# Maxima of an attention kernel: a chunk later in the projections, four steps of lead in place of six, and weight scales in three pieces

## What is computed

```python
def _tlin(x, w, s, b):
    return jnp.einsum('bsh,oh->bso', x, w) * s + b
q = split_heads(_tlin(x, w_q, s_q, b_q))      # k and v alike
scores = jnp.einsum('bhqd,bhkd->bhqk', q, k) / jnp.sqrt(jnp.float32(HEAD))
attn = jax.nn.softmax(scores, axis=-1)
ctx = jnp.einsum('bhqk,bhkd->bhqd', attn, v)
...
def fp4_quant_dequant(x):
    xb = x.reshape(shape[:-1] + (shape[-1] // BLOCK, BLOCK))
    scale = jnp.max(jnp.abs(xb), axis=-1, keepdims=True) / 6.0
    scale = jnp.maximum(scale, jnp.float32(1e-12))
    idx = jnp.searchsorted(_MID, jnp.abs(xb / scale))
    return (_GRID[idx] * jnp.sign(xb / scale) * scale).reshape(shape)
...
h = jax.nn.silu(fp4_linear(x, w_gate)) * fp4_linear(x, w_up)
x = _layernorm(x + fp4_linear(h, w_down), axis=-1)
```

## Time and profile before

| | us |
|---|---|
| median of 3 runs | 1972.64 |
| lowest, highest | 1971.41, 1978.06 |
| the profiled execution | 1978.5 |
| its span | 1976.7 |
| projections, up to the first attention maximum | 200.8 |
| attention steps with maxima (490) | 1179.0 |
| attention steps without maxima (22) | 52.5 |
| feed, up to the end | 544.4 |

### The profile page before, as it was taken

One profiled execution on the slowest core, in us unless ns is written; L12 is line 12 of the kernel. 1 busy time (PEld: TensorE's weight loads), 2 busy tenths in 40 slices (PEclk: granted clock), 3 DMA queues, 4 the chain that ended last, 5 costly groups with the idle time before them and its releaser, 6 DMA issues.

```text
span 1976.7 us, 43274 instructions
## 1 busy us (share of the span) xinstructions
PE 1921.4 (97%) x15934; PEld 1130.0 (57%) x15934; DVE 1846.1 (93%) x3237; ACT 1639.0 (83%) x3225; POOL 749.1 (38%) x747
## 2 busy tenths in 40 slices
PE   8999999999999999999999999999999999999998
PEld 7767444444444444444444444444478888888876
DVE  4798999999999999999999999999289999999997
ACT  5555889889898998989899898988967777777776
POOL 3000455666674362010001001000046666666785
PEclk9999999999999999999999999999999999999999
DMA  7985643354445435444543544452011111111210
GB/s 219 287 241 218 124 63 52 62 106 93 86 90 102 94 72 108 91 87 89 104 94 72 103 95 88 88 104 93 24 49 49 49 49 49 50 50 55 62 33 28
DMA packets 127200, 181.48 MB, mean 92 GB/s; under 512 B 37836, under 2 KB 82636, under 8 KB 126988
## 3 DMA queue, kind: packets, MB, share of 16 engines
q1 hardware_dynamic: 119308, 171.10, 37.3%
q10 hardware_dynamic: 7392, 7.34, 1.2%
q0 software_dynamic: 288, 0.27, 0.1%
HBM read 103.68 MB, written 73.40 MB: 90 GB/s over the span
## 4 chain that ended last, share of the span: by engine, by line
DVE 64%; PE 31%; issue 3%; DMA 1%; ACT 1%; SPq 0%; DVEq 0%; POOLq 0%; POOL 0%; ACTq 0%
DVE halfmax L1135 50%; PE ps L1401 11%; DVE halfmax L1130 7%; PE ps L1440 6%; PE ps L493 4%; PE ps L1389 2%; PE ps L505 2%; PE ps L1412 2%; PE ps L1045 1%; PE ps L1011 1%; PE ps L1448 1%; PE ps L480 1%; DVE room L1591 1%; PE ps L1457 1%; DVE room L1678 1%
## 5 line engine op out<-in xcount | busy, mean ns | idle before, releaser
L1096 ACT ACTIVATE room<-ps 128x512 f32<-128x512 f32 x2048 | 1085.0, 601 | 123.3 <-PE ps L1011 101.5
L1135 DVE TENSOR_REDUCE halfmax<-ps 128x1 f32<-128x512 f32 x1714 | 1040.3, 680 | 0.1
L1011 PE MATMUL ps<-qs,ks 50*128 50x512 f32 x2048 | 715.9, 448 | 2.4 <-DVE halfmax L1135 1.3
L986 PE MATMUL ps<-ks,qs 48*128 48x512 f32 x1960 | 667.0, 436 | 23.8 <-DVE halfmax L1130 22.4
L1045 PE MATMUL ps<-room,vals 128*17 128x256 f32 (+2 forms) x8192 | 578.2, 384 | 0.3 <-ACT craw L1104 0.3
L986 PEld LDWEIGHTS ps<-ks,qs 48*128 48x128 f32 x1960 | 314.2, 184 | 423.4 <-DVE halfmax L1135 308.1
L164 POOL CAST mrow<-turned_rows 128x32 fp32r<-128x32 f32 x32 | 6.7, 209 | 896.4 <-DVE turned_rows L159 688.5
L1011 PEld LDWEIGHTS ps<-qs,ks 50*128 50x128 f32 x2048 | 326.6, 184 | 22.8 <-ACT room L1096 14.5
L1045 PEld LDWEIGHTS ps<-room,vals 128*17 128x17 f32 x8192 | 167.3, 96 | 232.4 <-issue 167.6
L1401 PE MATMUL ps<-wguT,xqT 128*128 128x512 f32 (+1 forms) x1152 | 268.3, 386 | 3.9 <-DVE xqT L1631 3.9
L1401 PEld LDWEIGHTS ps<-wguT,xqT 128*128 128x128 f32 x1152 | 211.9, 189 | 51.8 <-issue 9.9
(11 more groups left out here) (119 smaller groups left out, 2202.1 us busy)
## 6 DMA issues: line engine op xcount, KB each, us to landing
qk_parts<-parts SPq DMA_DIRECT2D x64, 512.0 KB, 4.0
qs<-qk_parts SPq DMA_DIRECT2D x192, 128.0 KB, 4.4
ks<-qk_parts SPq DMA_DIRECT2D x192, 128.0 KB, 7.0
ctx_raw<-craw SPq DMA_DIRECT2D x64, 256.0 KB
ready<-passing SPq DMA_DIRECT2D x27, 512.0 KB, 6.2
pairs<-ready SPq DMA_DIRECT2D x27, 512.0 KB
out_dram<-fin SPq DMA_DIRECT2D x64, 128.0 KB, 2.1
xin<-in_L_attn_x_dram ACTq DMA_DIRECT2D x14, 512.0 KB, 5.6
```

What stands on the lines that cost most here:

```text
L986: nc.tensor.matmul(ps[:, MX + max_number(i, u, bank) % 4, :], qs[rows, i.slot(RING), pair, t * P:(t + 1) * P], ks[rows, i.slot(RING), pair ...
L1011: nc.tensor.matmul(ps[:, score_bank(i, s, n), :], ks[rows, slot, pair, kt * P:(kt + 1) * P], qs[rows, slot, pair, qh * BANK:(qh + 1) * BAN ...
L1096: nc.scalar.activation(prob[:, prob_slot(i, s), score_order(i, s)[n], :], ps[:, score_bank(i, s, n), :], ACT.Exp, scale=float(D) ** -0.5). ...
L1135: nc.vector.tensor_reduce(halfmax[:, i.slot(2), bank, column:column + 1], ps[:, at + bank, :], AX.X, ALU.max, negate=True).then_inc(max_re ...
```

## The change

AHEAD becomes 4 and MAX_FROM 6. So the projections hold maxima in chunks 6 to 15, 40 units in place of 44, LEAD becomes 8, TURN 14. In attention the maxima lead the scores by four steps: a group's maxima are complete after step 11 of the group before, the turn is in step 12, and BARE becomes 492. The weight scales are made in three pieces: half of the reduction in one chunk, the other half in the next, the two small operations in the third, each between `split_qk(i, 2)` and `take_max(i, 3)`. A job's load is a chunk ahead of its first piece, in chunks 6, 9 and 12, so the pieces fill chunks 7 to 15. The counts of `scales_done` follow (four a job). Line numbers behind the change are up to 14 higher.

```diff
@@ -47,7 +47,7 @@
-AHEAD = 6
+AHEAD = 4
 LEAD = 2 * AHEAD
@@ -298,11 +298,12 @@
-    MAX_FROM = S // C + 3
+    MAX_FROM = S // C + 4
     MAX_PER = 4
     TURN = MAX_FROM + MU // MAX_PER
+    SCALE_PIECES = 3
@@ -352,10 +353,17 @@
-    def scale_job(i):
-        return {MAX_FROM + 1: 0, MAX_FROM + 3: 1, NCH - 4: 2}.get(i.k)
+    def scale_load(i):
+        job, at = divmod(i.k - MAX_FROM, SCALE_PIECES)
+        return job if at == 0 and 0 <= job < 3 else None
+
+    def scale_piece(i):
+        job, piece = divmod(i.k - MAX_FROM - 1, SCALE_PIECES)
+        return (job, piece) if 0 <= job < 3 else None
@@ -397,14 +405,15 @@
-            wait(sp, scales_done, 3 * job)
+            if job > 0:
+                sp.wait_ge(scales_done, 4 * job - 2)
...
-            stage_weights(scale_job(i))
+            stage_weights(scale_load(i))
@@ -627,19 +636,24 @@
-        def weight_scales(job):
-            if job is None:
+        def weight_scales(which):
+            if which is None:
                 return
+            job, piece = which
...
-            dve.wait_ge(stage_in, 16 * (job + 1))
-            nc.vector.tensor_reduce(amax_w[0:np_, job, 0:nb], w, AX.X, ALU.max,
-                                    apply_absolute_value=True).then_inc(scales_done, 1)
-            dve.wait_ge(scales_done, 3 * job + 1)
+            if piece < 2:
+                if piece == 0:
+                    dve.wait_ge(stage_in, 16 * (job + 1))
+                blocks = slice(piece * nb // 2, (piece + 1) * nb // 2)
+                nc.vector.tensor_reduce(amax_w[0:np_, job, blocks], w[:, blocks], AX.X, ALU.max,
+                                        apply_absolute_value=True).then_inc(scales_done, 1)
+                return
+            dve.wait_ge(scales_done, 4 * job + 2)
...
@@ -678,12 +692,12 @@
             split_qk(i, 2)
+            weight_scales(scale_piece(i))
             take_max(i, 3)
...
             values(i, 1)
-            weight_scales(scale_job(i.plus(-1)))
@@ -1212,7 +1226,7 @@
-        pool.wait_ge(scales_done, 9)
+        pool.wait_ge(scales_done, 12)
```

More of the change, by code:

```diff
@@ L628, in split_qk @@
                                     ALU.subtract).then_inc(qk_split, 1)
-        def weight_scales(job):
-            if job is None:
+        def weight_scales(which):
+            if which is None:
                 return
+            job, piece = which
             w = staged(job).rearrange("p (n e) -> p n e", e=BLK)
             np_, nb = w.shape[0], w.shape[1]
-            dve.wait_ge(stage_in, 16 * (job + 1))
-            nc.vector.tensor_reduce(amax_w[0:np_, job, 0:nb], w, AX.X, ALU.max,
-                                    apply_absolute_value=True).then_inc(scales_done, 1)
-            dve.wait_ge(scales_done, 3 * job + 1)
+            if piece < 2:
[6 more added lines that the diff above has]
+            dve.wait_ge(scales_done, 4 * job + 2)
             nc.vector.tensor_scalar(amax_w[0:np_, job, 0:nb], amax_w[0:np_, job, 0:nb], 1.0 / 6.0, 1e-12,
                                     ALU.mult, ALU.max).then_inc(scales_done, 1)
-            dve.wait_ge(scales_done, 3 * job + 2)
+            dve.wait_ge(scales_done, 4 * job + 3)
             nc.vector.reciprocal(rcp_w[0:np_, job, 0:nb], amax_w[0:np_, job, 0:nb]).then_inc(scales_done, 1)
```

## The result

| | us |
|---|---|
| kernel before, median of 5 runs | 1976.09 (1971.41 to 1978.06) |
| changed kernel, median of 5 runs | 2001.37 (2000.60 to 2005.48) |
| ratio, with 95% interval | 1.0139 (1.0122 to 1.0157) |
| profiled execution of the changed kernel | 2000.88, span 1999.1 |

The kernel became slower, as forecast, but by 25 us and not by 14: 2001.4 lies above the range.

A forecast was written before the change was run, and what follows sets the result against it. VectorE, busy throughout attention, was taken as the bound. Projections -10.0, attention work 0, turns +22 and end of attention +2 gave +14 us, so 1972.6 became 1987 us, range 1968 to 1999.

The forecast's parts named there:

- The bound and its turn: Attention: VectorE has no idle time, so the late first score tile of a group costs it 0.74 us at 30 boundaries.
- landing: Turn in attention: the last of eight DMAs lands at 809.8, 6.4 us after the transposition starts.
- The projections: Projections: later maxima save 7.06 us in the first chunk with maxima, weight scales in pieces 2.96; together -10.0 us.
- The end of attention: After the last maxima: two weight transpositions slip behind tile 0's output projection, adding 2 us, between 0 and 4.
- the wait that was named: End of attention: tile 0's result is ready at about 1412.1, where ScalarE wants it at 1410.06.
- the turn's term: Attention turns: TensorE stands 1.2 us at each first tile, VectorE loses 0.74 at 30 boundaries, +22 us.
- The forecast's upper bound for the landing: Attention turns: landing at 810.2, by the output stores' 2.1 us; wait 1.6, loss 1.15 a boundary, +35 us.
- the base: Whole kernel: +14 us added to the median 1972.6, the profiled execution lying 6 us above it.
- the hidden stall: Rival, attention turns: cushion over 1.2 us, so only -10 + 2 is left, 1964.6 us; chance 0.16.
- the partly hidden one: Rival, attention turns: loss of 0.1 to 0.45 us a boundary, within 6 us of before; chance 0.13.
- The long landing: Rival, attention turns: DMAs land later, +25 to +40 us, to some 2005; chance 0.09.
- The later stores: Rival, projections: stores catch up with ScalarE and the projections gain less, 3 us more in any case; no chance of its own.

The follow-up runs named there:

- The kernel with four tiles in front of the wait: Changed kernel, with TensorE making four unused score-sized tiles before its wait for the maxima at each turn; 1996.4 us, ratio 1.0104.
- the pieces alone: Changed kernel with AHEAD back at 6 and maxima from chunk 5, leaving only the weight scales in pieces; 1971.0 us, ratio 0.9984.
- The kernel in which this wait is taken away: Changed kernel with two of the eight DMAs issued by GpSimd and the weights' transpositions made earlier; 1964.8 us, ratio 0.9943.
- the split kernel: Changed kernel with two of the eight DMAs of a turn issued by GpSimd, six by SyncE; 1965.6 us, ratio 0.9958.
- the second profile: Changed kernel run again, unchanged, for another profile; 1999.8 us, span 1998.0.
- the run with the ninth DMA: Changed kernel with one more DMA ahead of the eight, which the first score tile also waits for; 2079.2 us, ratio 1.0531.
- the lead alone: Kernel before with only AHEAD = 4, maxima still from chunk 5 and weight scales whole; 2004.9 us, ratio 1.0161.
- part 0 early: Changed kernel with SyncE sending the first part's four DMAs as soon as GpSimd has made that part; 1985.9 us.
- the kernel with five steps: Kernel before with only AHEAD = 5; 1977.5 us, ratio 1.001.

## Why the prediction missed its number

**Right.** The bound and its turn: VectorE busy all through attention, a chain of 6.38 us against four steps, TensorE's wait of 1.2, VectorE's loss of 0.74 (0.73 to 0.94 at the ordinary turns, 0.79 in the mean). Over all 30 turns, less the falls, it is 25.3 us where 22 were forecast: 0.79 rather than 0.74 at an ordinary turn, and 0.3 to 0.6 more at the four longer chains. The kernel with four tiles in front of the wait, which has no fall, has the same 25.4.

The *landing*: 8 issues of 0.545 us, the last of which lands 1.6 us after its start, by the chain of waits (821.91 to 823.51). The Trainium skill (DMA: Bandwidth & Descriptors, Anatomy of one DMA, on the path of GpSimd's DMAs) gives a fixed 2.0 us, most of it the write receipt, and by it, as an estimate, the sum would have been 10 us higher. SyncE issues these eight, and the trace has 1.6, so the rows were the better guide; that the total came out above the page's sum all the same has another reason.

The projections: from the point where the change begins to act they are 10.1 us shorter, 10.0 was forecast, and both of TensorE's waits of 1.30 are gone; the pieces alone gain 3.7 us, 3.0 were forecast.

The end of attention costs 2.3 us more than two steps fewer should, 2 was forecast, and the wait that was named is there:

```profile
1432.85 0.20 ACT L1490 ACTIVATE centre<-mv 128x1 f32<-128x1 f32 x1 [1.46 <-POOL rstd L1709]
```

The number is partly luck. The kernel in which this wait is taken away gains 1.4 us at the place, and the split kernel, which has the wait, is 1.4 us shorter here than the changed one: its granted clock stays at 1.00 in this stretch, where the changed kernel has 0.93 and the kernel before 0.97. So a lower clock has a part in the 2.3 us, and the forecast didn't have it.

**Wrong, the turn's term.** It priced TensorE's 1.2 us of standing still by its length alone: "VectorE loses 1.2 - 0.48 = 0.74". The text spoke of the granted clock only for the projections, where a wait of 2.96 was followed by a slow stretch. The same thing at the turns, where a new wait of over 1 us was being forecast thirty times, was left out, so its price was put at nothing without a reason. Measured: two falls in this profile. The groups behind them are 3.3 and 4.4 us longer than the ordinary ones, but these turns have longer chains too; against the same turns in the kernel with four tiles, which has no fall, they are 2.7 and 4.0, **6.7 us**. In the second profile two falls make 1.3 + 4.1 = 5.4, and by the medians keeping TensorE at work gains 5.0. And the price of more wait is not 0.54 us a turn but 2.6: the distance to 2079 us was one DMA. The forecast's upper bound for the landing (TensorE standing for 1.6) gave +35 us for the turns and +27 in all; the run with the ninth DMA, where it stands for 1.87 (817.24 to 819.11), is 104 us above the kernel before.

**Wrong, the base.** "The profiled execution lies 6 us above the median; the difference is the same against either." It isn't. That execution had the 2.96 us wait, the change takes just this wait away, and the 7.06 us that the forecast took for it are the most that any of five executions shows; three of them have 3.7 to 4.1. Against its own span the forecast of +14 misses the measured +22.4 by 8.4: falls +6.7, turns +3.3, the earlier start of this execution -1.3, the rest -0.3. The other 6 us of the miss are the median, and they have more than one source. 2.1 of them are the median itself: it was taken from 3 runs, and those of 13 to 15 later ones are 1974.7. In the other 3.8 lie the first chunk, 3.0 to 3.4 us longer than in those three executions, and the late start of that execution. How much of it each makes isn't shown. A part that varies from execution to execution has to be taken away from the same base from which its gain is read.

The rivals: the hidden stall, and the partly hidden one, did not come. The long landing gave 2005 us, which is near, but the landing was not long, so that nearness is chance. The later stores did not catch up with ScalarE.

## What to carry to other kernels

Shortening the lead of a chain has a threshold: compare the chain, from its first instruction to the landing of its last DMA, with the work that covers it, and expect no cost on one side of it. If TensorE is going to stand still for 1 us or more, price also the slow clock that may follow; here a few tiles that nobody uses in front of the wait were cheaper than the stall's aftermath (2013.2 against 2079.2), and dividing the chain's DMAs over two queues took the wait away. If one execution is profiled, ask first in what it differs from the median, and whether the change touches just that.

## What the runs showed of the hardware

The granted clock fell to 1.2 GHz behind single waits of TensorE in the midst of a stage that is otherwise without a gap. At the turns of the kernels with four steps of lead (the changed one twice, the lead alone, part 0 early) it fell behind none of the waits up to 0.87 us (by the bracket), behind one of six between 1.00 and 1.12, and behind all five from 1.13 to 1.36; with the ninth DMA behind 28 of 30, which lie between 1.28 and 1.71. In the changed kernel's profile it stayed low for some 7 and 10 us; a fall cost VectorE 1.3 to 4.1 us.

The length of one wait doesn't decide it alone. Where the maxima end, TensorE's wait of 1.42 us at 1405.2 in the changed kernel, and of 1.40 at 1370.3 in the split one, left the clock at 1.00 behind them; one of 1.46 at 1379.0 in the kernel with five steps was followed by 0.52. And at the entry to attention the clock was low for 3.4 us from 190.4 on in the changed kernel's second profile, behind waits of 0.20 and 0.45. What else counts wasn't tried.

The last of a row of eight DMAs from SBUF to SBUF landed 1.6 us after its issue began. GpSimd issued two in 1.22 us, a little slower than SyncE with 0.545 each, and beside it.
